# A recurrent layer whose states move from PSUM to SBUF, with rows staged by channel group and weights loaded in pieces

## The chip, the cores and the metric

The kernel runs on one NeuronCore of a Trainium2 chip. The metric is device time in microseconds. A core has five engines that run side by side: TensorE (PE, matrix products), VectorE (DVE), ScalarE (ACT), GpSimd (POOL) and SyncE (SP, which here only issues DMAs). They wait for each other through semaphores. SBUF is the working memory; PSUM is the small memory into which TensorE writes, and GpSimd does not touch it.

## What is computed

Two transformer-like layers over 32 sequences of 192 tokens (64 from images, 128 from text), 256 channels wide. The first has attention and a ternary feed-forward net. The second has a recurrent mixer with 512 inner channels and then a mixture of 8 experts. The change touches the recurrent mixer and the loads of the experts' weights. From the reference, cut to the mixer:

```python
xz = einsum('btd,ed->bte', x, Win)
xi, z = split(xz, 2, axis=-1)
lam = exp(-C * softplus(omega) * sigmoid(xi @ Wl.T + bl))
v = xi @ Wv.T + bv
h0 = xi[:, 0]
def step(h_prev, inp):
    x_t, v_t, lam_t = inp
    vh = sum(v_t * h_prev, axis=-1, keepdims=True)
    vv = sum(v_t * v_t, axis=-1, keepdims=True)
    Qh = h_prev - 2.0 * v_t * (vh / vv)
    h = lam_t * Qh + (1.0 - lam_t) * x_t
    return (h, h)
# h = all states, one after the other over t
out = einsum('bti,di->btd', silu(z) * h, Wout)
```

Every time step needs the state of the step before it, so the 192 steps form one chain.

## The kernel before

The program has three parts, one after the other: `part_a` (embedding and the first layer), `part_b` (the recurrent mixer) and `part_c` (the experts). The change is in `part_b`, apart from one number in `part_c`.

`part_b` works in 48 tiles of 4 time steps. A tile is 32 sequences x 4 steps = 128 rows. Every engine runs the same loop over `i`, from -5 to 50, and in pass `i` it does what each stage of the pipeline needs: tile `i` is in the scan, tile `i + 3` is being projected, tile `i - 1` is being turned into outputs.

The stages of tile `j` are these. TensorE projects the normed rows onto four things of 512 columns each (`l`, `v`, `xi`, `z`), each split in high and low parts for precision. ACT and DVE make from them four rows of 512 values: `U` (the scaled v), `LAM` (the decay), `DRIVE` and `GATE`, and write them to the tile `B_stage` in SBUF. There a partition is a row (sequence and step). The scan needs another layout: a partition is a sequence and one of 4 groups of 128 channels, and the steps lie behind each other. So SP issues four DMAs of 256 KB, one per channel group, from `B_stage` to the ring `B_scan_in` (4 tiles deep).

The scan itself runs on DVE and TensorE. For step `t` DVE does four operations on 128 x 128 values:

- `products(t)`: U times the previous state, summed along the free axis into one partial dot per partition (`B_partial_dots`, L1187),
- `decayed(t)`: LAM times the previous state (L1189),
- `driven(t)`: minus DRIVE (L1192),
- `stepped(t)`: plus `B_decayed_u` times the full dot (L1203).

Between the first and the last of them TensorE sums the partial dots over the four channel groups with one small product (L1296). The first three operations of step `t + 1` are issued right behind the last of step `t` (function `ahead`), so the scan comes in groups of four DVE operations: `stepped(t)`, `products(t+1)`, `decayed(t+1)`, `driven(t+1)`. Between the groups DVE does the other work of the pass: B_residual (L1215) and the GATE row (L1221) after the first, B_log_decay (L1231) and the statistics (L1237, L1240) after the second, B_y_lo (L1245) and B_x_lo (L1252) after the third, the DRIVE row (L1265) after the fourth. All of these have at most one input in SBUF that is wide; the other comes from PSUM.

The states lie in PSUM, in two banks that take turns (`STATE + j % 2`). When a tile is through, ACT copies its four states to `B_states` in SBUF (L1110), and GpSimd multiplies them with the gate into `B_y` (L1036). GpSimd also makes `B_decayed_u` = LAM x U for the next tile (L1048), and some operations on one value per partition. All engines take their work strictly in the written order, so one that waits holds up all that is behind it.

The experts' first two weight matrices and the small constants of `part_c` are loaded during `part_b`, in pass `TT - 18` = 30, all at one point of the SP queue.

Of the kernel before, what the change touches and what calls it, by code (L numbers as in the profile page):

```python
# [846 lines left out]
def part_b(nc, W, E, io, consts):  # L847
# [3 lines left out]
    with ExitStack() as ctx:  # L851
# [28 lines left out]
        stage = sb("B_stage", [P, 2, 4, DI])  # L880
# [11 lines left out]
        TURN, OUT, STATE, DOT = 3, 4, 5, 7  # L892
# [4 lines left out]
        def state(j, k):  # L897
            return ps[:, STATE + j % 2, k * P:(k + 1) * P]
# [62 lines left out]
        def _(sp):  # L961
# [13 lines left out]
            for i in range(FIRST, LAST):  # L975
                if i == TT - 18:
                    for a, b in ((E.b_up, io["up_bias"]), (E.b_dn, io["down_bias"])):
                        sp.dma_start(a[:], b).then_inc(E.s["const_in"], 16)
# [712 lines left out]
```

## Time and profile before

| what | value |
|---|---|
| median of 3 runs | 997.94 us (995.04 to 998.17) |
| the profiled execution, own time | 999.17 us |
| its span | 997.4 us |
| PE busy | 942.3 us, 94% |
| DVE busy | 785.9 us, 79% |
| ACT busy | 594.5 us, 60% |
| POOL busy | 542.2 us, 54% |
| TensorE clock over the span | 0.983 of full |
| moved by DMA | 96.34 MB in 135878 packets |

The rows come from one profiled execution; its own time is 1.8 us above its span. Busy time of matrix products overlaps, since they are pipelined, so a busy TensorE is not one at its peak. Durations of neighbouring DVE operations overlap a little too: an operation that need not wait starts some 0.08 us before the end of the one ahead of it.

### The profile page before, as it was taken

The numbers are of one execution on the slowest core, as the hardware profiler recorded it, in microseconds if no ns is written. First come the engines' busy times: TensorE is split into PE (matmuls) and PEld (weight loads), VectorE is DVE, ScalarE is ACT, GpSimd is POOL, SyncE is SP. The second block draws the span as 40 slices with busy tenths as digits, with TensorE's granted clock in tenths as the row PEclk, the third lists the DMA queues.
The fourth block names the chain that finished last, engine by engine and source line by source line (L and its number), as shares of the span: only waits on it lengthen the run. The fifth ranks groups of instructions, "written<-read, shape, count | busy, mean of one in ns | idle before, by whom it ended". The sixth has DMA issues, their size and how long they took to land. (4 is left out here: it accounts for less than half of the span.)

```text
span 997.4 us, 19802 instructions
## 1 busy us (share of the span) xinstructions
PE 942.3 (94%) x6006; PEld 844.9 (85%) x6006; DVE 785.9 (79%) x2396; ACT 594.5 (60%) x1181; POOL 542.2 (54%) x662
## 2 busy tenths in 40 slices
PE   6889999999999999988799999999998999997998
PEld 6789999999999999875588888888887888876887
DVE  4877777777777777664499999999997889995776
ACT  1366666666666666563567676777664666752541
POOL 4256666666666666344355455555543446542663
PEclk9999999999999999899899999999999899999999
DMA  6001111111111141003799999999999999993210
GB/s 221 17 27 43 44 43 43 42 42 42 42 42 42 42 149 32 17 17 111 89 149 156 156 156 154 156 154 155 155 154 173 145 153 145 150 143 76 98 64 22
DMA packets 135878, 96.34 MB, mean 97 GB/s; under 512 B 12270, under 2 KB 130166, under 8 KB 135158
## 3 DMA queue, kind: packets, MB, share of 16 engines
q1 hardware_dynamic: 134262, 91.20, 53.4%
q0 software_dynamic: 1536, 4.20, 1.4%
q8 instruction: 36, 0.59, 0.3%
q14 instruction: 44, 0.36, 0.2%
HBM read 31.91 MB, written 13.11 MB: 45 GB/s over the span
## 5 line engine op out<-in xcount | busy, mean ns | idle before, releaser
L334 POOL TENSOR_TENSOR gelu_lo<-gelu_out,gelu_hi 128x384 fp32r<-128x384 f32 x124 | 145.6, 1200 | 34.0 <-DVE gelu_hi L549 32.1
L1036 POOL TENSOR_TENSOR B_y<-B_scan_in,B_states 128x512 f32<-128x512 f32 x48 | 61.8, 1288 | 97.8 <-ACT B_states L1110 97.8
L752 PE MATMUL psAB<-ternary_down,gelu_hi 128*128 128x256 f32 x384 | 96.7, 290 | 4.9 <-POOL gelu_lo L334 4.0
L688 PE MATMUL psAB<-x2T_hi,ternary_up 128*128 128x384 f32 x256 | 94.9, 371 | 2.5 <-DVE residual L678 2.3
L752 PE MATMUL psAB<-ternary_down,gelu_lo 128*128 128x256 f32 x384 | 93.3, 282 | 0.0
L688 PE MATMUL psAB<-x2T_lo,ternary_up 128*128 128x384 f32 x256 | 87.9, 343 | 0.0
L1284 PE MATMUL psAB<-Win_hi,B_x_hi 128*128 128x512 f32 x192 | 83.5, 435 | 0.0
L1296 PEld LDWEIGHTS psAB<-B_partial_dots,B_minus_same_batch 128*128 128x128 f32 x384 | 65.3, 191 | 18.2 <-DVE B_partial_dots L1187 9.2
L752 PEld LDWEIGHTS psAB<-ternary_down,gelu_hi 128*128 128x128 f32 x384 | 72.2, 188 | 8.9 <-POOL gelu_lo L334 7.5
L1203 DVE SCALAR_TENSOR_TENSOR psAB<-B_decayed_u,psAB 128x128 f32<-128x128 f32 x192 | 68.0, 354 | 12.7 <-PE psAB L1296 11.5
L1284 PE MATMUL psAB<-Win_hi,B_x_lo 128*128 128x512 f32 x192 | 75.7, 394 | 0.0
L1284 PE MATMUL psAB<-Win_lo,B_x_hi 128*128 128x512 f32 x192 | 75.2, 392 | 0.0
L1048 POOL TENSOR_TENSOR B_decayed_u<-B_scan_in 128x512 f32<-128x512 f32 x48 | 62.0, 1291 | 24.0 <-DMA B_scan_in<-B_stage 16.8
L752 PEld LDWEIGHTS psAB<-ternary_down,gelu_lo 128*128 128x128 f32 x384 | 72.5, 189 | 0.0
L1042 POOL TENSOR_TENSOR B_v_scale<-B_half_vv,half_powers 128x1 f32<-128x1 f32 x48 | 26.3, 548 | 83.9 <-ACT B_v_squared L1131 79.3
L403 ACT ACTIVATE gelu_out<-psAB 128x384 f32<-128x384 f32 x128 | 62.6, 489 | 13.6 <-PE psAB L688 13.3
L1187 DVE CUSTOM_DVE_ANT_0 B_products<-B_scan_in,psAB 128x128 f32<-128x128 f32 x192 | 55.2, 287 | 19.0 <-DVE psAB L1203 7.8
L1192 DVE TENSOR_TENSOR psAB<-psAB,B_scan_in 128x128 f32<-128x128 f32 x192 | 57.4, 299 | 6.5
L568 DVE TENSOR_TENSOR gelu_sq_sum<-gelu_sq_sum,gelu_sq 128x384 f32<-128x384 f32 x105 | 61.1, 582 | 1.7
L1296 PE MATMUL psAB<-B_partial_dots,B_minus_same_batch 128*128 128x1 f32 x384 | 55.0, 212 | 7.3 <-DVE B_partial_dots L1187 7.1
L688 PEld LDWEIGHTS psAB<-x2T_hi,ternary_up 128*128 128x128 f32 x256 | 49.2, 192 | 11.6 <-ACT gelu_out L403 7.4
L1309 PE MATMUL psAB<-Wout_hi,B_y_hi 128*128 128x256 f32 x192 | 55.3, 288 | 2.7 <-DVE B_y_lo L1245 1.5
(267 smaller groups left out, 3330.4 us busy)
## 6 DMA issues: line engine op xcount, KB each, us to landing
B_scan_in<-B_stage SPq DMA_DIRECT2D x192, 256.0 KB, 6.6
patches<-in_patches SPq DMA_DIRECT2D x16, 384.0 KB, 3.1
B_residual<-layer_out SPq DMA_DIRECT2D x48, 128.0 KB, 3.5
out_dram<-B_residual SPq DMA_DIRECT2D x48, 128.0 KB, 2.8
layer_out<-residual SPq DMA_DIRECT2D x32, 128.0 KB, 1.8
raw_Win<-in_experts SPq DMA_DIRECT2D x4, 768.0 KB, 4.4
raw_Wl<-in_experts SPq DMA_DIRECT2D x4, 768.0 KB, 4.1
layer_out<-residual SPq DMA_DIRECT2D x32, 64.0 KB, 2.0
```

The source lines that it names most:

```text
L334: nc.gpsimd.tensor_tensor(act_l[:, k, :], act[:, k % DEEP, :], act_h[:, k, :].bitcast(F32), ALU.subtract).then_inc(s["ffn_lo"], 1)
L403: nc.scalar.activation(act[:, k % DEEP, :], ps[:, 6 + k % 2, 0:GT], ACT.Gelu).then_inc(s["gelu_done"], 1)
L568: nc.vector.tensor_tensor(sqsum[:], sqsum[:], sq[:, k % DEEP, :], ALU.add).then_inc(s["sqsum_done"], 1)
L688: last = nc.tensor.matmul(out, a, b, start=(n == 0), stop=(n == len(terms) - 1))
L752: last = nc.tensor.matmul(ps[:, 6 + k // 2, (k % 2) * D:(k % 2 + 1) * D], x[:, c, k * P:(k + 1) * P], dn_w[:, c, :], start=(c == 0 and x i ...
L1036: nc.gpsimd.tensor_tensor(y[:, j % 2], ring[:, j % R_RING, :, GATE, :], hs[:, j % 2], ALU.mult).then_inc(s["y"], 1)
L1048: nc.gpsimd.tensor_tensor(lu[:, j % 2], ring[:, j % R_RING, :, LAM, :], ring[:, j % R_RING, :, U, :], ALU.mult).then_inc(s["lu"], 1)
L1192: nc.vector.tensor_tensor(state(j, k), state(j, k), ring[:, j % R_RING, k, DRIVE, :], ALU.subtract).then_inc(s["scan"], 1)
L1203: nc.vector.scalar_tensor_tensor(out=state(i, k), in0=lu[:, i % 2, k, :], scalar=dot[:, t % 2:t % 2 + 1], in1=state(i, k), op0=ALU.mult, o ...
L1284: last = nc.tensor.matmul(out, a, b, start=(not biased and ks[0] == 0 and n == 0), stop=(ks[-1] == DC - 1 and n == len(terms) - 1), skip_g ...
L1296: nc.tensor.matmul(dot[:, t % 2:t % 2 + 1], minus[:], part[:, t % 2:t % 2 + 1], start=True, stop=True).then_inc(s["dot"], 1)
L1309: last = nc.tensor.matmul(ps[:, OUT, 0:D], *terms[n], start=(n == 0), stop=(n == len(terms) - 1))
```

## The change

There are three edits.

1. *Rows staged by channel group.* `B_stage` is laid out as group, row kind, channel instead of row kind, channel. The writes to it go through a view (`by_group`), and each of the four DMAs reads 2 KB in a piece per partition instead of four pieces of 512 B.
2. *Experts' inputs in small pieces.* The loads that stood at one point of the SP queue are spread over passes 22 to 36, one or two per pass, behind that pass's transfer to the scan; each weight matrix comes in four pieces of 192 KB.
3. *States in SBUF.* `state(j, k)` now is a part of `B_states`. ACT's copy and its semaphore go. GpSimd's B_y waits for the last step of the tile itself, and `ahead` waits for `y` before it writes over a tile of states. The two `tensor_tensor` of the scan become `scalar_tensor_tensor` with a factor of 1.0.

```diff
-        stage = sb("B_stage", [P, 2, 4, DI])
+        stage = sb("B_stage", [P, 2, IC, 4, P])
...
         def state(j, k):
-            return ps[:, STATE + j % 2, k * P:(k + 1) * P]
+            return hs[:, j % 2, k, :]
...
+        def by_group(ap):
+            return ap.rearrange("p (g c) -> p g c", g=IC)
...
-                if i == TT - 18:
-                    for a, b in ((E.b_up, io["up_bias"]), (E.b_dn, io["down_bias"])):
-                        sp.dma_start(a[:], b).then_inc(E.s["const_in"], 16)
...
-                    sp.wait_ge(s["w_lo"], 3)
-                    sp.wait_ge(s["m_ps"], 2)
-                    for e in range(2):
-                        sp.dma_start(E.raw[e], io["experts"][e]).then_inc(E.s["raw_in%d" % e], 16)
...
                     for g in range(IC):
                         sp.dma_start(ring[g * NB:(g + 1) * NB, j % R_RING].rearrange("b r w c -> b (r w c)"),
-                                     stage[:, j % 2, :, g * P:(g + 1) * P]).then_inc(arrived[j % 4], 16)
+                                     stage[:, j % 2, g, :, :].rearrange("p w c -> p (w c)")).then_inc(arrived[j % 4], 16)
+
+
+                if i == TT - 26:
+                    sp.dma_start(E.b_up[:], io["up_bias"]).then_inc(E.s["const_in"], 16)
+                    sp.dma_start(E.b_dn[:], io["down_bias"]).then_inc(E.s["const_in"], 16)
...
+                if i in range(TT - 19, TT - 11):
+                    if i == TT - 19:
+                        sp.wait_ge(s["w_lo"], 3)
+                        sp.wait_ge(s["m_ps"], 2)
+                    e, n = divmod(i - (TT - 19), 4)
+                    cols = slice(n * 6 * D // 4, (n + 1) * 6 * D // 4)
+                    sp.dma_start(E.raw[e][:, cols], io["experts"][e][:, cols]).then_inc(E.s["raw_in%d" % e], 16)
...
-                    pool.wait_ge(s["hs"], j + 1)
+                    pool.wait_ge(s["scan"], stepped(4 * j + 3))
...
-                if has(i - 1):
-                    j = i - 1
-                    sc.wait_ge(s["scan"], decayed(4 * j + 4) if j + 1 < TT else stepped(4 * j + 3))
-                    wait(sc, s["y"], j - 1)
-                    nc.scalar.activation(hs[:, j % 2].rearrange("p a b -> p (a b)"), ps[:, STATE + j % 2, :],
-                                         ACT.Copy).then_inc(s["hs"], 1)
...
-                    wait(v, s["hs"], j - 1)
+                    wait(v, s["y"], j - 1)
...
-                nc.vector.tensor_tensor(state(j, k), ring[:, j % R_RING, k, LAM, :], previous(j, k),
-                                        ALU.mult).then_inc(s["scan"], 1)
+                nc.vector.scalar_tensor_tensor(out=state(j, k), in0=ring[:, j % R_RING, k, LAM, :], scalar=1.0,
+                                               in1=previous(j, k), op0=ALU.mult, op1=ALU.mult).then_inc(s["scan"], 1)
                 v.wait_ge(s["scan"], decayed(t))
-                nc.vector.tensor_tensor(state(j, k), state(j, k), ring[:, j % R_RING, k, DRIVE, :],
-                                        ALU.subtract).then_inc(s["scan"], 1)
+                nc.vector.scalar_tensor_tensor(out=state(j, k), in0=state(j, k), scalar=1.0,
+                                               in1=ring[:, j % R_RING, k, DRIVE, :], op0=ALU.mult,
+                                               op1=ALU.subtract).then_inc(s["scan"], 1)
```

The order of the work on DVE stays. What its operations read and write changes, and one wait. These are the rows of DVE where one tile of the scan ends and the next begins, with the semaphores that each waits for. psAB is PSUM, all other names are in SBUF; ISA is the operation of L1187. Before:

```order
L1203 SCALAR_TENSOR_TENSOR psAB<-B_decayed_u,psAB 128x128 [waits B_dot,B_scan]
L1187 ISA B_products,B_partial_dots<-B_scan_in,psAB 128x128 [waits B_scan,B_hs,B_arrived3]
L1187 ISA B_partial_dots 128x1
L1189 TENSOR_TENSOR psAB<-B_scan_in,psAB 128x128
L1192 TENSOR_TENSOR psAB<-psAB,B_scan_in 128x128 [waits B_scan]
L1265 SCALAR_TENSOR_TENSOR B_stage<-B_stage,psAB 128x512 [waits B_xi,B_lam]
```

And of the changed kernel:

```order
L1205 SCALAR_TENSOR_TENSOR B_states<-B_decayed_u,psAB,B_states 128x128 [waits B_dot,B_scan]
L1188 ISA B_products,B_partial_dots<-B_scan_in,B_states 128x128 [waits B_scan,B_y,B_arrived3]
L1188 ISA B_partial_dots 128x1
L1190 SCALAR_TENSOR_TENSOR B_states<-B_scan_in,B_states 128x128
L1193 SCALAR_TENSOR_TENSOR B_states<-B_states,B_scan_in 128x128 [waits B_scan]
L1267 SCALAR_TENSOR_TENSOR B_stage<-B_stage,psAB 128x4x128 [waits B_xi,B_lam]
```

Each of the four operations of a step read one wide tensor from PSUM and one from SBUF before, and reads two from SBUF now (psAB in the first row is the dot, one value per partition). The wait for B_hs became one for B_y.

The second place is the SP queue in pass 30, where the loads for the experts stand. Before, from the transfer of the pass ahead to that of the pass itself:

```order
L1020 DMA B_scan_in<-B_stage 32x16x128 x4
L978 DMA C_up_bias<-in_up_bias 128x32
L978 DMA C_down_bias<-in_down_bias 8x256
L984 DMA C_picked<-in_picked 128x2 x2
L984 DMA C_picked<-in_picked 64x2 x4
L984 DMA C_routing<-in_routing 128x8 x2
L984 DMA C_routing<-in_routing 64x8 x4
L988 DMA raw_Win<-in_experts 128x1536
L988 DMA raw_Wl<-in_experts 128x1536
L1010 DMA out_dram<-B_residual 32x4x256
L964 DMA B_residual<-layer_out 128x1x256
L1020 DMA B_scan_in<-B_stage 32x16x128 x4
```

And of the changed kernel, at the same pass:

```order
L1010 DMA B_scan_in<-B_stage 32x4x512 x4
L1028 DMA raw_Win<-in_experts 128x384
L1000 DMA out_dram<-B_residual 32x4x256
L967 DMA B_residual<-layer_out 128x1x256
L1010 DMA B_scan_in<-B_stage 32x4x512 x4
L1028 DMA raw_Win<-in_experts 128x384
```

Sixteen transfers that stood ahead of one tile's inputs are gone from there; one small piece stands behind each tile's inputs instead.

## Rows read from the trace of the kernel before

**Rows 1.** Busy time by engine (operations), clock, DMA share, GB/s, mid-layer.

```profile
600.00:700.00 100.00, 100.00 (x589) 86.09 (x587) 92.51 (x329) 69.44 (x141) 50.35 (x83) 1.00 1.05 155
```

**Rows 2.** Timeline of DVE, one tile: start, length, operation, idle before.

```profile
640.45 0.36 DVE L1203 SCALAR_TENSOR_TENSOR psAB<-B_decayed_u,psAB 128x128 f32<-128x128 f32 x1 [0.21 <-PE psAB L1296]
...
641.38 0.30 DVE L1192 TENSOR_TENSOR psAB<-psAB,B_scan_in 128x128 f32<-128x128 f32 x1
...
644.79 0.35 DVE L1203 SCALAR_TENSOR_TENSOR psAB<-B_decayed_u,psAB 128x128 f32<-128x128 f32 x1
...
646.85 0.35 DVE L1203 SCALAR_TENSOR_TENSOR psAB<-B_decayed_u,psAB 128x128 f32<-128x128 f32 x1
647.37 0.29 DVE L1187 CUSTOM_DVE_ANT_0 B_products<-B_scan_in,psAB 128x128 f32<-128x128 f32 x1 [0.17 <-DVE psAB L1203]
...
647.59 0.29 DVE L1189 TENSOR_TENSOR psAB<-B_scan_in,psAB 128x128 f32<-128x128 f32 x1
647.91 0.30 DVE L1192 TENSOR_TENSOR psAB<-psAB,B_scan_in 128x128 f32<-128x128 f32 x1
648.12 0.68 DVE L1265 SCALAR_TENSOR_TENSOR B_stage<-B_stage,psAB 128x512 f32<-128x512 f32 x1
649.01 0.36 DVE L1203 SCALAR_TENSOR_TENSOR psAB<-B_decayed_u,psAB 128x128 f32<-128x128 f32 x1 [0.21 <-PE psAB L1296]
```

**Rows 3.** Timeline of GpSimd in the same tile.

```profile
641.46 1.28 POOL L1036 TENSOR_TENSOR B_y<-B_scan_in,B_states 128x512 f32<-128x512 f32 x1 [2.37 <-ACT B_states L1110]
...
644.81 1.29 POOL L1048 TENSOR_TENSOR B_decayed_u<-B_scan_in 128x512 f32<-128x512 f32 x1
...
647.48 0.19 POOL L1060 TENSOR_TENSOR B_shift<-B_minus_mean,B_rstd 128x1 f32<-128x1 f32 x1
```

**Rows 4.** Groups by shape (busy us, mean ns), then B_y's line (min/median/max ns).

```profile
L568 DVE TENSOR_TENSOR gelu_sq_sum<-gelu_sq_sum,gelu_sq 128x384 f32<-128x384 f32 x105 | 61.1, 582 | 1.7
L1192 DVE TENSOR_TENSOR psAB<-psAB,B_scan_in 128x128 f32<-128x128 f32 x192 | 57.4, 299 | 6.5
L549 DVE CAST gelu_hi<-gelu_out 128x384 fp32r<-128x384 f32 x80 | 28.3, 369 | 3.9 <-ACT gelu_out L403 3.8
...
L1036 POOL TENSOR_TENSOR B_y<-B_scan_in,B_states x48: 1270/1287/1299, 505.2 to 910.8; 128x512 f32<-128x512 f32 x48
```

**Rows 5.** Timelines of POOL and DVE where both use SBUF, three places.

```profile
66.89 3.23 POOL L334 TENSOR_TENSOR gelu_lo<-gelu_out,gelu_hi 128x384 fp32r<-128x384 f32 x2 [1.26 <-DVE gelu_hi L549]
...
419.92 1.26 POOL L334 TENSOR_TENSOR gelu_lo<-gelu_out,gelu_hi 128x384 fp32r<-128x384 f32 x1 [3.81 <-DVE gelu_hi L549]
...
419.76 0.55 DVE L568 TENSOR_TENSOR gelu_sq_sum<-gelu_sq_sum,gelu_sq 128x384 f32<-128x384 f32 x1
420.23 1.17 DVE L549 CAST gelu_hi<-gelu_out 128x384 fp32r<-128x384 f32 x1
...
926.91 3.48 POOL L1422 TENSOR_TENSOR C_w_lo<-raw_Win,C_w_hi 128x1536 fp32r<-128x1536 f32 x1
...
929.47 2.08 DVE L1523 SCALAR_TENSOR_TENSOR C_glu<-C_up,C_silu 128x512 f32<-128x512 f32 x2
```

**Rows 6.** Timelines of SP's queue and DVE, and two us by windows.

```profile
754.48 3.50 SPq L984 DMA_DIRECT2D C_routing<-in_routing  x6
...
760.83 3.65 SPq L1020 DMA_DIRECT2D B_scan_in<-B_stage  x4
...
760.21 0.36 DVE L1203 SCALAR_TENSOR_TENSOR psAB<-B_decayed_u,psAB 128x128 f32<-128x128 f32 x1 [0.18 <-PE psAB L1296]
...
773.12 0.29 DVE L1187 CUSTOM_DVE_ANT_0 B_products<-B_scan_in,psAB 128x128 f32<-128x128 f32 x1 [6.15 <-DMA B_scan_in<-B_stage]
...
785.68 0.36 DVE L1203 SCALAR_TENSOR_TENSOR psAB<-B_decayed_u,psAB 128x128 f32<-128x128 f32 x1 [0.38 <-PE psAB L1296]
...
773.00:775.00 2.00, 0.62 (x3) 0.57 (x3) 1.45 (x6) 1.88 (x4) 1.62 (x3) 0.50 1.24 169
```

**Rows 7.** Timeline of GpSimd late in the layer.

```profile
837.56 3.51 POOL L1064 TENSOR_TENSOR C_w_lo<-raw_Win,C_w_hi 128x1536 fp32r<-128x1536 f32 x1
```

More of the change, by code:

```diff
@@ L891, in part_b @@
         MERGE = (0, 1, 2, 3)
[L892 removed]
+        TURN, OUT, DOT = 3, 4, 7
         def bank(what, j):
@@ L908, in part_b @@
                 stats aggr ve rstd shift applied xT x_hi x_lo l v xi z tanh_l log_decay lam vsq rs u drive
-                tanh_z gate lu scan dot hs y yT y_hi y_lo wout res""".split():
+                tanh_z gate lu scan dot y yT y_hi y_lo wout res""".split():
             s[name] = ctx.enter_context(nc.semaphore("B_" + name))
@@ L1020, in _ @@
                         sp.dma_start(ring[g * NB:(g + 1) * NB, j % R_RING].rearrange("b r w c -> b (r w c)"),
-                                     stage[:, j % 2, :, g * P:(g + 1) * P]).then_inc(arrived[j % 4], 16)
+                                     stage[:, j % 2, g, :, :].rearrange("p w c -> p (w c)")).then_inc(arrived[j % 4], 16)
+                if i == TT - 26:
+                    sp.dma_start(E.b_up[:], io["up_bias"]).then_inc(E.s["const_in"], 16)
+                    sp.dma_start(E.b_dn[:], io["down_bias"]).then_inc(E.s["const_in"], 16)
+                if i in range(TT - 25, TT - 19):
+                    q, lo, hi, q_in, lo_in = ((0, 0, P, 0, 0), (2, 0, P, 3, 0), (1, 0, 64, 1, 64), (1, 64, P, 2, 0),
+                                              (3, 0, 64, 1, 0), (3, 64, P, 2, 64))[i - (TT - 25)]
+                    for a, b in ((E.picked, io["picked"]), (E.weights, io["routing"])):
+                        sp.dma_start(a[lo:hi, q, :], b[lo_in:lo_in + hi - lo, q_in, :]).then_inc(E.s["const_in"], 16)
+                if i in range(TT - 19, TT - 11):
[5 more added lines that the diff above has]
+                    sp.dma_start(E.raw[e][:, cols], io["experts"][e][:, cols]).then_inc(E.s["raw_in%d" % e], 16)
         @block.gpsimd
@@ L1155, in _ @@
                     sc.wait_ge(s["rs"], j + 1)
[L1156 removed]
+                    nc.scalar.activation(stage[:, j % 2, :, U, :], by_group(ps[:, bank("v", j), :]), ACT.Copy,
                                          scale=rs[:, j % 2:j % 2 + 1]).then_inc(s["u"], 1)
                     sc.wait_ge(s["log_decay"], j + 1)
[L1159 removed]
+                    nc.scalar.activation(stage[:, j % 2, :, LAM, :], by_group(u2[:]), ACT.Exp).then_inc(s["lam"], 1)
                     if has(j + 1):
@@ L1220, in _ @@
                     v.wait_ge(s["tanh_z"], j + 1)
-                    nc.vector.scalar_tensor_tensor(out=stage[:, j % 2, GATE, :], in0=th_z[:], scalar=1.0,
-                                                   in1=ps[:, bank("z", j), :], op0=ALU.add,
+                    nc.vector.scalar_tensor_tensor(out=stage[:, j % 2, :, GATE, :], in0=by_group(th_z[:]), scalar=1.0,
+                                                   in1=by_group(ps[:, bank("z", j), :]), op0=ALU.add,
                                                    op1=ALU.mult).then_inc(s["gate"], 1)
@@ L1260, in _ @@
                     if j == 0:
-                        nc.vector.tensor_scalar(stage[:, 0, LAM, :], stage[:, 0, LAM, :], first[:], None,
+                        nc.vector.tensor_scalar(stage[:, 0, :, LAM, :], stage[:, 0, :, LAM, :], first[:], None,
                                                 ALU.mult).then_inc(s["first_ready"], 1)
@@ L1264, in _ @@
                     v.wait_ge(s["xi"], j + 1)
-                    nc.vector.scalar_tensor_tensor(out=stage[:, j % 2, DRIVE, :], in0=stage[:, j % 2, LAM, :], scalar=1.0,
-                                                   in1=ps[:, bank("xi", j), :], op0=ALU.subtract,
+                    nc.vector.scalar_tensor_tensor(out=stage[:, j % 2, :, DRIVE, :], in0=stage[:, j % 2, :, LAM, :], scalar=1.0,
+                                                   in1=by_group(ps[:, bank("xi", j), :]), op0=ALU.subtract,
                                                    op1=ALU.mult).then_inc(s["drive"], 1)
```

10 lines of the change are left out of this document (2 added, 8 removed).

## The prediction, made before the changed kernel had run

> **What bounds the kernel now.** I read the page's busy table first, then one long stretch of the recurrent layer by windows, then one tile of it as a timeline on the vector engine and on GpSimd, then the places where DVE and GpSimd both want SBUF, and last the one place where the scan stops. The recurrent layer is 48 tiles of 4 time steps. In a stretch in its middle TensorE is busy 100.00 of 100 us and DVE 92.51 [rows 1]. Two engines are full, and the reader is to see which has slack. A tile lasts 649.01 - 640.45 = 8.56 us (48 of them are 411 of the 997 us), and within it DVE waits for TensorE once, 0.21 us, in front of the tile's first step [rows 2]. Everything else on DVE is one chain: step, product, decay, subtraction, then an operation of another kind, four times over. So TensorE sets the pace, and DVE follows with only 0.21 us to spare per tile. Whatever adds more than that to DVE's tile sets a new pace.
>
> GpSimd is half idle. Per tile it runs two wide operations, B_y at 641.46 and B_decayed_u at 644.81, and some tiny ones [rows 3]. The 48 B_y took 1270 to 1299 ns [rows 4]: nothing DVE did beside them mattered, and all that DVE did beside them had at most one input in SBUF, the other in PSUM.
>
> **What the change adds: two SBUF inputs.** The states move from PSUM to SBUF. Then all four operations of a step read two SBUF tensors: 16 operations per tile that meet B_y and B_decayed_u, which read SBUF too. The trace shows what such a meeting costs [rows 5]. At 929.47 DVE starts two C_glu operations (512 wide, both inputs in SBUF) while GpSimd is inside a C_w_lo that ends at 926.91 + 3.48 = 930.39. A 512-wide operation of this kind lasts 0.68 us [rows 2], and a next one starts some 0.08 before its end, so the pair should take 1.28; it took 2.08. DVE stood for 0.80 us, until about 0.12 us before GpSimd's end. It did not run slower beside GpSimd, it stood. The other way round, at 66.89 two GpSimd operations took 3.23 us together where at 419.92 one took 1.26. So one engine holds the port for nearly its whole operation: 1.29 - 0.13 = 1.16 us for B_y or B_decayed_u.
>
> The Trainium skill says this in the page "SBUF — State Buffer", section "Who interferes with whom": a DVE instruction with two SBUF inputs and a GpSimd instruction that reads SBUF shut each other out, and the first holds the pair for the whole instruction. The trace agrees but for the last 0.13 us; with the whole 1.29 the sum below would be 48 x 0.13 = 6 us larger.
>
> **Who gets the port.** At 419.76 a DVE addition (0.55) ran and a CAST followed at 420.23; GpSimd had asked at 419.92, and the CAST took 1.17 us where its group's mean is 369 ns [rows 4, 5]. If the addition frees the port 0.13 before its end at 420.31, GpSimd slipped into a gap of 0.05 us. In the scan chain the gaps are wider: the decay at 647.59 frees the port at 647.75 and the subtraction comes at 647.91, 0.16 later; step 3 ends at 647.20 and the product comes at 647.37 [rows 2]. So I take it that GpSimd gets in inside the chain, and a DVE operation behind it stands for 1.16 - 0.16 = 1.0 us.
>
> **The sum per tile.** *B_y.* Before, it waited for ACT's copy and began 1.01 us into the tile, beside operations that read PSUM. Now it waits for step 3 itself, which ends at 647.20, while GpSimd is free from 647.67 at the latest [rows 3]. So it is asked for inside the chain (product, decay, subtraction at 647.37 to 648.21), and costs 1.0 us. Lower bound: it has to wait until the subtraction ends, holds 648.08 to 649.24, and the next step, due at 649.01, loses 0.23. *B_decayed_u.* It starts at 644.81, and step 2 at 644.79: a tie today. In front of step 2 lie 1.1 us of DVE work that uses no second SBUF input. Once DVE is the late one, B_decayed_u, timed by TensorE and ACT, comes earlier against DVE and hides most of its 1.16 there. I take 0.2; bounds 0, and 1.0 if it always falls inside a chain. *Spare time:* 0.21 us is given back. *The operations themselves:* 384 wide with both inputs in SBUF, outside meetings, the group at line 568 has a mean of 582 ns including some meetings; the PSUM forms have 299 ns at 128 and 680 at 512 [rows 2, 4], so 550 at 384. I see no gain from SBUF and take 0 for the three-operand form too, since the 680 is of that form. Together 1.0 + 0.2 - 0.2 = 1.0 us per tile, 48 us in all (bounds 0.0 and 1.8: 0 and 86 us).
>
> The Trainium skill's page "VectorE: DVE Perf Modes", section "The TRN2 errata", puts the fixed part at 58 cycles from SBUF and 120 from PSUM. By it each of the 16 operations would be an estimated 0.065 us shorter, 1.0 us per tile, and the block would be paid back in full. The rows do not show it, and so it stands as a rival.
>
> **What the change removes.** The experts' weights now come as one load of 192 KB in each of eight tiles instead of two of 768 KB and fourteen small ones in one go. Today the SP queue is busy with the small ones past 754.48 + 3.50, the inputs of the next tiles are issued behind them at 760.83, and DVE waits 6.15 us for them at 773.12 [rows 6]. TensorE then comes back at a granted clock of 0.50, the lower level (1.2 GHz). From the first step at 760.21 to the one at 785.68 two tiles take 25.47 instead of 17.12 us: 8.35 lost, of which the wait is 6.15 and the rest the low clock and the catching up. With pieces, and with B_stage sent as 2 KB instead of 512 B runs, I take all of it as gained: -8.35 (bound: 6.15 of it at least). The DMA share in the steady stretch, 1.05 [rows 1], falls, but no one waits for it there: worth 0. The copy on ACT (48 times) is hidden behind B_y's slack: 0. Added: C_w_lo (3.51 us at 837.56 [rows 7]) now holds the port too, some 3.4 us against at most 1.1 of DVE work that does not need it, +2.3; from that go some 1.3 us for hitches there that now hide behind DVE: +1.
>
> Sum: 999.17 (the profiled execution: span 997.4 and 1.8 around it) + 48 - 8.35 + 1 = 1039.8. The profiled execution lies 1.2 above the median 997.94, so 1038.6, say **1038 us**.
>
> **Rivals.**
> *B: GpSimd gets the port only between the groups of four.* For it: at 66.89 GpSimd was held off over several DVE operations in a row [rows 5]; against it: the CAST at 420.23, and wider gaps here. Then B_y costs 0.23, B_decayed_u up to 0.7 where it arrives ahead of step 2, say 0.4; less 0.21 it is 0.45 per tile, 21 us: 998 + 21 - 7 = 1012 (1003 to 1028).
> *C: faster.* The block is paid by something: shorter operations from SBUF, or both GpSimd operations landing in the port-free stretches. Place: the first step of each tile; price: the stall's 8.35 us against 48 tiles, so it decides at 8.35/48 = 0.17 us of net delay per tile. Below that the kernel is faster, down to 998 - 9 = 989. Against it: the spare 0.21, B_y's lower bound 0.23 and the tie at 644.8.
> *D: the stall stays* (the pieces collide with other loads) and the block comes: 1047.
> *E: they cancel*, 995 to 1001.
>
> **Chances.** A (the forecast, own range 1020 to 1060) 0.52, B 0.25, C 0.14, D 0.04, E 0.05. Within 0.3% (3 us) is about what a measurement here can tell from no change. Slower: A + B + D = 0.81; same 0.05; faster 0.14. The range leaves out C and E (0.19): 1003 to 1060.
>
> **What would show it.** Right: in the middle of the layer a tile of about 9.5 us instead of 8.56; TensorE waiting for B_partial_dots once or twice per tile; single DVE scan operations of 1.2 to 1.4 us among those of 0.3, always beside B_y or B_decayed_u; B_y starting within 0.1 us of step 3's end or as soon as the shift is done; no wait for B_scan_in near 766 us; TensorE's clock at its upper level there. Wrong: scan operations of 0.30 us throughout beside a running B_y (then C); long ones only as first of a group (then B); or GpSimd operations grown to 2.5 us while DVE keeps its pace, which would mean that DVE always wins the port and only GpSimd pays.

## The result, and the profile after

The changed kernel takes 1065.14 us (median of 4 runs, 1061.57 to 1069.31); the kernel before took 997.85 beside it. The ratio is 1.0682 with a 95% interval of 1.0628 to 1.0737: slower by 6.8%. The forecast was 1038 with a range of 1003 to 1060. The sign and the kind of loss came as forecast; one of the two meetings at the port was priced far too low, and so the loss is 67 us and not 40. The profiled execution, from which the rows of this section come, took 1068.38 us, 3.2 above the median; its mean granted clock was 0.979, where the two quicker runs had 0.989.

The same stretch of the layer as in [rows 1], by windows (busy time of each engine, its operations, clock, DMA share, GB/s):

```profile
600.00:700.00 100.00, 93.45 (x499) 72.31 (x498) 95.59 (x277) 53.79 (x110) 43.95 (x68) 1.00 0.79 129
```

TensorE has fallen from 100.00 to 93.45 us of 100, and in the same time it does 499 products instead of 589. DVE has risen to 95.59 with fewer operations (277 for 329). The granted clock is 1.00 in both, the upper level (2.4 GHz), so the clock plays no part in this stretch. The profile page's groups of the vector operations of the scan and of the weight load behind them say where the time sits (busy us, mean ns, then idle time before and what ended it):

```profile
L1188 DVE CUSTOM_DVE_ANT_0 B_products<-B_scan_in,B_states 128x128 f32<-128x128 f32 x192 | 105.4, 549 | 13.0 <-DVE B_states L1205 7.9
L1298 PEld LDWEIGHTS psAB<-B_partial_dots,B_minus_same_batch 128*128 128x128 f32 x384 | 58.7, 191 | 65.1 <-DVE B_partial_dots L1188 63.3
L1205 DVE SCALAR_TENSOR_TENSOR B_states<-B_decayed_u,psAB,B_states 128x128 f32<-128x128 f32 x192 | 102.6, 534 | 2.0 <-PE psAB L1298 1.3
```

A mean of 549 ns hides two sorts of operation. The vector operations that touch B_states and GpSimd's B_y, by line (min/median/max ns), show that most are as short as before, and that GpSimd's own operations are not longer:

```profile
L1188 DVE CUSTOM_DVE_ANT_0 B_products<-B_scan_in,B_states x192: 284/292/1355, 493.3 to 975.9; 128x128 f32<-128x128 f32 x192
L1190 DVE SCALAR_TENSOR_TENSOR B_states<-B_scan_in,B_states x192: 279/285/1373, 493.5 to 976.1; 128x128 f32<-128x128 f32 x192
L1193 DVE SCALAR_TENSOR_TENSOR B_states<-B_states,B_scan_in x192: 291/292/1416, 493.8 to 976.4; 128x128 f32<-128x128 f32 x192
L1205 DVE SCALAR_TENSOR_TENSOR B_states<-B_decayed_u,psAB,B_states x192: 341/350/3400, 494.2 to 977.2; 128x128 f32<-128x128 f32 x192
L1043 POOL TENSOR_TENSOR B_y<-B_scan_in,B_states x48: 1262/1292/1361, 502.0 to 977.7; 128x512 f32<-128x512 f32 x48
```

The timeline of DVE, from the first step of one tile (644.32) over its step 3 (651.47) and the first step of the next tile (654.39) to the step 2 of that one (658.73), and that of GpSimd beside it:

```profile
644.32 0.35 DVE L1205 SCALAR_TENSOR_TENSOR B_states<-B_decayed_u,psAB,B_states 128x128 f32<-128x128 f32 x1
...
651.47 0.35 DVE L1205 SCALAR_TENSOR_TENSOR B_states<-B_decayed_u,psAB,B_states 128x128 f32<-128x128 f32 x1
651.99 1.34 DVE L1188 CUSTOM_DVE_ANT_0 B_products<-B_scan_in,B_states 128x128 f32<-128x128 f32 x1 [0.17 <-DVE B_states L1205]
...
653.79 0.68 DVE L1267 SCALAR_TENSOR_TENSOR B_stage<-B_stage,psAB 128x512 f32<-128x512 f32 x1
654.39 0.35 DVE L1205 SCALAR_TENSOR_TENSOR B_states<-B_decayed_u,psAB,B_states 128x128 f32<-128x128 f32 x1
...
658.73 1.09 DVE L1205 SCALAR_TENSOR_TENSOR B_states<-B_decayed_u,psAB,B_states 128x128 f32<-128x128 f32 x1
```

```profile
651.90 1.29 POOL L1043 TENSOR_TENSOR B_y<-B_scan_in,B_states 128x512 f32<-128x512 f32 x1 [0.58 <-DVE B_states L1205]
657.86 0.55 POOL L1049 TENSOR_TENSOR B_v_scale<-B_half_vv,half_powers 128x1 f32<-128x1 f32 x1 [4.67 <-ACT B_v_squared L1132]
658.38 1.30 POOL L1055 TENSOR_TENSOR B_decayed_u<-B_scan_in 128x512 f32<-128x512 f32 x1
```

B_y starts 0.08 us after step 3 ends (651.82) and 0.09 before the product; the product then takes 1.34 instead of 0.29: a block of 1.05, as the time for which a DVE operation stands is called here. B_decayed_u starts at 658.38, 0.35 before step 2, and step 2 takes 1.09 instead of 0.35: a block of 0.74. Together 1.79; the 0.21 that DVE used to wait at the tile's first step [rows 2] comes off: 1.58. The tile has in fact grown from 8.55 to 10.08 us, by 1.53, and stays there from the third tile on, apart from three tiles around ACT's C_w_hi and GpSimd's C_w_lo and the last two.

### The profile page after: what moved, and what is told of

Read it like the earlier page. It is cut to its first block and busy times, and to the rows that moved or that the text cites. A ratio compares the mean times of both kernels' runs of the same rounds, so it can differ in the third digit from the quotient of the medians.

```text
span 1066.6 us, 19714 instructions
## 1 busy us (share of the span) xinstructions
PE 981.3 (92%) x6006; PEld 843.4 (79%) x6006; DVE 869.9 (82%) x2396; ACT 569.5 (53%) x1133; POOL 548.9 (51%) x662
## 5 line engine op out<-in xcount | busy, mean ns | idle before, releaser
L1188 DVE CUSTOM_DVE_ANT_0 B_products<-B_scan_in,B_states 128x128 f32<-128x128 f32 x192 | 105.4, 549 | 13.0 <-DVE B_states L1205 7.9
L1298 PEld LDWEIGHTS psAB<-B_partial_dots,B_minus_same_batch 128*128 128x128 f32 x384 | 58.7, 191 | 65.1 <-DVE B_partial_dots L1188 63.3
L1205 DVE SCALAR_TENSOR_TENSOR B_states<-B_decayed_u,psAB,B_states 128x128 f32<-128x128 f32 x192 | 102.6, 534 | 2.0 <-PE psAB L1298 1.3
L1112 ACT ACTIVATE psAB<-B_channel_rows 128x512 f32<-128x512 f32 x48 | 28.9, 602 | 114.5 <-DVE B_stage L1267 114.5
L1298 PE MATMUL psAB<-B_partial_dots,B_minus_same_batch 128*128 128x1 f32 x384 | 68.6, 248 | 22.7 <-DVE B_partial_dots L1188 20.8
L1311 PE MATMUL psAB<-Wout_hi,B_y_hi 128*128 128x256 f32 x192 | 58.7, 306 | 19.0 <-DVE B_x_lo L1254 16.4
L1311 PEld LDWEIGHTS psAB<-Wout_hi,B_y_hi 128*128 128x128 f32 x192 | 36.9, 192 | 37.8 <-DVE B_y_lo L1247 37.0
L1193 DVE SCALAR_TENSOR_TENSOR B_states<-B_states,B_scan_in 128x128 f32<-128x128 f32 x192 | 57.2, 298 | 6.6
```

The source lines that it names most:

```text
L1188: nc.vector.tensor_tensor_reduce(prod[:], ring[:, j % R_RING, k, U, :], previous(j, k), 1.0, 0.0, ALU.mult, ALU.add, part[:, t % 2:t % 2 + ...
L1205: nc.vector.scalar_tensor_tensor(out=state(i, k), in0=lu[:, i % 2, k, :], scalar=dot[:, t % 2:t % 2 + 1], in1=state(i, k), op0=ALU.mult, o ...
L1298: nc.tensor.matmul(dot[:, t % 2:t % 2 + 1], minus[:], part[:, t % 2:t % 2 + 1], start=True, stop=True).then_inc(s["dot"], 1)
L1311: last = nc.tensor.matmul(ps[:, OUT, 0:D], *terms[n], start=(n == 0), stop=(n == len(terms) - 1))
```

## Experiments

Each was compared with the kernel before on the same chip. Diffs are against the changed kernel unless said otherwise, and line numbers differ by a few from kernel to kernel. First the results at a glance; the tile is that of the middle of the layer. The kernel before took 997.85 us beside the changed kernel and 994.82 to 995.60 beside the others, so the ratios say more than the differences of the times. narrow_y and the three whose names begin with tiny leave out part of the computation.

| kernel | us | ratio to before, 95% interval | tile, us |
|---|---|---|---|
| before | 997.85 | 1 | 8.55 |
| changed | 1065.14 | 1.0682 [1.0628, 1.0737] | 10.08 |
| stage_only | 995.15 | 1.0000 [0.9987, 1.0013] | 8.55 |
| pieces_only | 988.68 | 0.9937 [0.9917, 0.9957] | 8.55 |
| stage_and_pieces | 989.11 | 0.9933 [0.9915, 0.9951] | 8.55 |
| states_only | 1067.10 | 1.0713 [1.0694, 1.0731] | 10.09 |
| two_operand | 1064.16 | 1.0694 [1.0676, 1.0712] | 10.09 |
| narrow_y | 1043.44 | 1.0463 [1.0441, 1.0484] | 9.68 |
| tiny_y | 1042.52 | 1.0463 [1.0440, 1.0485] | 9.68 |
| tiny_decayed_u | 1028.64 | 1.0336 [1.0311, 1.0361] | 9.34 |
| tiny_both | 991.92 | 0.9969 [0.9952, 0.9986] | 8.59 |
| y_placed | 1042.92 | 1.0480 [1.0455, 1.0504] | 9.67 |
| both_placed | 1019.42 | 1.0227 [1.0198, 1.0257] | 8.7 to 9.8 |
| y_and_u_late | 998.35 | 1.0038 [1.0025, 1.0052] | 8.67 |

### Which edit does what

**stage_and_pieces**: edits 1 and 2 of the section on the change, without edit 3. As a diff against the changed kernel it puts the states back:

```diff
-            return hs[:, j % 2, k, :]
+            return ps[:, STATE + j % 2, k * P:(k + 1) * P]
...
-                    pool.wait_ge(s["scan"], stepped(4 * j + 3))
+                    pool.wait_ge(s["hs"], j + 1)
...
```

> The kernel before with the first two edits alone: rows staged by channel group, loads in pieces; the states stay in PSUM and ACT copies them. Theory P (the port: the loss comes only from DVE operations with two SBUF inputs meeting GpSimd's wide ones): no loss is left and the stall near 766 us is gone, so about 8 us less than before, 990 us, tiles of 8.56 us throughout. Theory S (the new staging layout or the pieces cost DVE or the DMA queue time, and the states only part of it): clearly above 998 us.

**states_only**: edit 3 alone, the same lines the other way round in the kernel before.

> The kernel before with the third edit alone: states in SBUF, B_y waits for the last step, no copy on ACT. P: the tile of 10.09 us as in the changed kernel, and the stall at the experts' loads is hidden or partly hidden behind the slower pace, so 1065 to 1073 us. S: well below 1060.

Measured: 989.11 and 1067.1. All of the loss is edit 3. The two tiles at the experts' loads take 11.43 and 11.26 instead of 10.09 in states_only, where they took 14.75 and 10.72 before. So beside a scan that DVE paces, the pile of loads costs only 1.34 + 1.17 = 2.5 us.

**stage_only** and **pieces_only** take edits 1 and 2 apart. Against the kernel before, the first has

```diff
-        stage = sb("B_stage", [P, 2, 4, DI])
+        stage = sb("B_stage", [P, 2, IC, 4, P])
...
-                                     stage[:, j % 2, :, g * P:(g + 1) * P]).then_inc(arrived[j % 4], 16)
+                                     stage[:, j % 2, g, :, :].rearrange("p w c -> p (w c)")).then_inc(arrived[j % 4], 16)
...
```

and the second has the loads at `i in range(TT - 19, TT - 11)` in place of those at `i == TT - 18`.

> The kernel before with the first edit alone (rows staged by channel group, 2 KB runs). If the stall near 766 us is a matter of DMA time, the shorter transfers shrink it: the experts' two loads of 768 KB still stand ahead of the scan's inputs, so some 2 to 6 us of the 8.35 are gained, 992 to 996 us. If it is a matter of the fifteen issues on SP's queue ahead of it, nothing: 998 us.

> The kernel before with the second edit alone (loads in pieces, 512 B runs stay). The DMA share in the steady stretch is 1.05 already, so pieces of 192 KB add about 5% per tile for eight tiles. Either they are hidden in the slack of 6.6 us to landing (990 us), or each of eight tiles is late by up to 0.5 us (990 to 994 us). No stall at 766 us in both.

What DVE waited for between 740 and 800 us (total, times, longest), in stage_only:

```profile
DVE B_products L1190 <- DMA B_scan_in<-B_stage: 6.0, 1, 6.0
DVE psAB L1206 <- PE psAB L1299: 2.7, 7, 1.1
```

and in pieces_only:

```profile
DVE psAB L1206 <- PE psAB L1299: 1.4, 7, 0.2
DVE B_products L1190 <- DVE psAB L1206: 1.2, 7, 0.2
```

The wait of 6.0 us stays with the staging alone and is gone with the pieces alone. Staging by channel group cuts the packets of the execution from 135878 to 62150 and the DMA share in the middle of the layer from 1.05 to 0.91, and the time does not move: 1.0000, interval ±0.0013. The whole gain of 0.6% is the pieces'. So the shorter transfers did not shrink the stall, and the second reading of stage_only's expectation stands. The SP queue of the kernel before shows it too:

```profile
746.13 3.78 SPq L1020 DMA_DIRECT2D B_scan_in<-B_stage  x4
749.96 0.63 SPq L978 DMA_DIRECT2D C_up_bias<-in_up_bias  x1
```

The transfers to the scan were issued 8.55 us apart (737.58, 746.13), so the next was due at 754.68. The sixteen loads kept the queue from 749.96 to 759.07, and it came at 760.83 [rows 6], 6.15 late. That the two loads of 768 KB (issued in 0.96 us of this) also delay the data is not excluded: no run takes them apart from the fourteen small ones.

**two_operand**: the decay and the subtraction as `tensor_tensor` again.

```diff
-                nc.vector.scalar_tensor_tensor(out=state(j, k), in0=ring[:, j % R_RING, k, LAM, :], scalar=1.0,
-                                               in1=previous(j, k), op0=ALU.mult, op1=ALU.mult).then_inc(s["scan"], 1)
+                nc.vector.tensor_tensor(state(j, k), ring[:, j % R_RING, k, LAM, :], previous(j, k),
+                                        ALU.mult).then_inc(s["scan"], 1)
...
-                nc.vector.scalar_tensor_tensor(out=state(j, k), in0=state(j, k), scalar=1.0,
-                                               in1=ring[:, j % R_RING, k, DRIVE, :], op0=ALU.mult,
-                                               op1=ALU.subtract).then_inc(s["scan"], 1)
+                nc.vector.tensor_tensor(state(j, k), state(j, k), ring[:, j % R_RING, k, DRIVE, :],
+                                        ALU.subtract).then_inc(s["scan"], 1)
```

> The changed kernel with the two operations of the scan that were turned into scalar_tensor_tensor written as tensor_tensor again, on the same SBUF operands. P: the form is of no account, both have two SBUF inputs; 1065 us within 3, operations within 15 ns of 285. Rival F (the three-operand form is what is slow, or what helps): a change of over 5 us one way or the other.

The tile is 10.09 and the time 1064.16: the form is of no account.

### Taking the meetings away

**narrow_y**: B_y for one of the four steps.

```diff
+            nc.gpsimd.memset(y[:], 0.0)
...
-                    nc.gpsimd.tensor_tensor(y[:, j % 2], ring[:, j % R_RING, :, GATE, :], hs[:, j % 2],
+                    nc.gpsimd.tensor_tensor(y[:, j % 2, 0:1], ring[:, j % R_RING, 0:1, GATE, :], hs[:, j % 2, 0:1],
                                             ALU.mult).then_inc(s["y"], 1)
```

> The changed kernel, in which GpSimd multiplies only one of the four steps of a tile with its gate (B_y 128 wide instead of 512; the other three quarters of B_y stay zero). Its length should fall from 1.29 to about 0.43 us, from the 1.005 us of 384 and 1.29 of 512 elements, so its hold of the port to 0.30. P: the product that stands behind it takes 0.5 instead of 1.34 us, the tile 9.25 instead of 10.09, the kernel about 1065 - 40 = 1025 us. S (states in SBUF are slow for DVE by themselves): 1065 us, since nothing on DVE changes.

Its tile is 9.68, 0.41 shorter, where 0.84 was expected, and the time 1043.44 and not 1025. B_y (0.46 us) does block only 0.22. But step 2 and B_decayed_u now come at the same moment. DVE, then GpSimd:

```profile
653.00 1.44 DVE L1207 SCALAR_TENSOR_TENSOR B_states<-B_decayed_u,psAB,B_states 128x128 f32<-128x128 f32 x1
```

```profile
653.00 1.30 POOL L1057 TENSOR_TENSOR B_decayed_u<-B_scan_in 128x512 f32<-128x512 f32 x1
```

GpSimd wins the tie and step 2 takes 1.44 instead of 1.09: -0.83 + 0.35 = -0.48. With the 0.07 that DVE waits again at the tile's first step (B_stage ends at 648.66, the step starts at 648.65 and not 0.08 before that end) this is the -0.41 seen. Half of what is taken off one meeting comes back at the other. So the two were then removed singly and together, by making 16 of the 512 columns only. Tiny_both has both parts of this diff, and tiny_y and tiny_decayed_u have one each:

```diff
+            nc.gpsimd.memset(y[:], 0.0)
+            nc.gpsimd.memset(lu[:], 0.0)
...
-                    nc.gpsimd.tensor_tensor(y[:, j % 2], ring[:, j % R_RING, :, GATE, :], hs[:, j % 2],
-                                            ALU.mult).then_inc(s["y"], 1)
+                    nc.gpsimd.tensor_tensor(y[:, j % 2, 0, 0:16], ring[:, j % R_RING, 0, GATE, 0:16],
+                                            hs[:, j % 2, 0, 0:16], ALU.mult).then_inc(s["y"], 1)
...
-                    nc.gpsimd.tensor_tensor(lu[:, j % 2], ring[:, j % R_RING, :, LAM, :], ring[:, j % R_RING, :, U, :],
-                                            ALU.mult).then_inc(s["lu"], 1)
+                    nc.gpsimd.tensor_tensor(lu[:, j % 2, 0, 0:16], ring[:, j % R_RING, 0, LAM, 0:16],
+                                            ring[:, j % R_RING, 0, U, 0:16], ALU.mult).then_inc(s["lu"], 1)
```

> The changed kernel with B_y and B_decayed_u made by GpSimd for 16 of their 512 columns only; the rest of both is zero, so most of these two products is left out. Theory (the two meetings at the port are all of the loss): the blocks of 1.05 and 0.74 us shrink to at most 0.1 each, the vector engine's tile is 10.08 - 1.05 - 0.74 = 8.29 to 8.5 us, TensorE sets the pace again at 8.55, and the time is that of the kernel with the loads in pieces alone, 988.7 (986 to 993). Rival 1 (states in SBUF cost something besides the meetings, on ACT, TensorE or in the vector operations): tile above 8.65, more than 995. Rival 2 (the three-operand operations from SBUF are quicker): the same time, but the vector engine waits for TensorE by about 1.2 us per tile (0.21 before plus 16 x 0.065) instead of 0.1 to 0.4.

> The changed kernel with B_y alone made for 16 of its 512 columns; the rest of B_y is zero. If the blocks simply added up, the tile would be 10.08 - 1.05 = 9.03 us and the time 1065 - 50 = 1015. By what the narrow B_y showed, B_decayed_u then meets step 2 head on and takes 1.05 to 1.09 there instead of 0.74: tile 9.35 to 9.45, time 1030 to 1035.

> The changed kernel with B_decayed_u alone made for 16 of its 512 columns; the rest of B_decayed_u is zero. B_y still starts within 0.1 us of step 3's end whatever comes before it, so its block stays 1.05 and the term of B_decayed_u goes whole: tile 10.08 - 0.74 = 9.34 (9.3 to 9.45), time 1065 - 35 = 1030 (1027 to 1034). This is the size that the forecast gave to B_y alone. Rival: with B_decayed_u gone another meeting grows (B_y held longer): above 1040.

| | B_decayed_u gone | B_decayed_u whole |
|---|---|---|
| B_y gone | 8.59 us, 991.9 | 9.68 us, 1042.5 |
| B_y whole | 9.34 us, 1028.6 | 10.08 us, 1065.1 |

With both gone, TensorE is busy 100.00 us of 100 again although all states are in SBUF (tiny_both, by windows):

```profile
600.00:700.00 100.00, 100.00 (x584) 85.66 (x584) 92.36 (x326) 62.94 (x127) 26.12 (x80) 1.00 0.93 153
```

So the two meetings are all of the loss in the steady stretch but for 0.04 us per tile. What is left against pieces_only is 3.2 us: these 0.04, and C_w_lo, which still blocks a step. DVE waits 0.19 us for TensorE at the tile's first step and not 1.2, so rival 2 falls too. B_y alone costs 0.75 over 8.59, B_decayed_u alone 1.09, both together 1.49: they do not add up. tiny_decayed_u came as expected. tiny_y missed: a tile of 9.68 and 1042.5 where 9.35 to 9.45 and 1030 to 1035 stood. Its step 2 takes 1.45 and DVE waits 0.20 for TensorE again at the tile's first step; I had left that wait out of the sum. DVE:

```profile
651.97 1.45 DVE L1207 SCALAR_TENSOR_TENSOR B_states<-B_decayed_u,psAB,B_states 128x128 f32<-128x128 f32 x1
...
656.42 0.68 DVE L1269 SCALAR_TENSOR_TENSOR B_stage<-B_stage,psAB 128x512 f32<-128x512 f32 x1
657.30 0.36 DVE L1207 SCALAR_TENSOR_TENSOR B_states<-B_decayed_u,psAB,B_states 128x128 f32<-128x128 f32 x1 [0.20 <-PE psAB L1300]
```

and GpSimd, over two tiles:

```profile
651.97 1.30 POOL L1057 TENSOR_TENSOR B_decayed_u<-B_scan_in 128x512 f32<-128x512 f32 x1
...
661.13 0.55 POOL L1051 TENSOR_TENSOR B_v_scale<-B_half_vv,half_powers 128x1 f32<-128x1 f32 x1 [5.33 <-ACT B_v_squared L1134]
661.65 1.29 POOL L1057 TENSOR_TENSOR B_decayed_u<-B_scan_in 128x512 f32<-128x512 f32 x1
```

### Placing the meetings

**y_placed**: B_y waits for the decay of the next tile's second step, so that it is held until the subtraction ends and lies under B_residual and B_stage.

```diff
-                    pool.wait_ge(s["scan"], stepped(4 * j + 3))
+                    pool.wait_ge(s["scan"], decayed(4 * j + 5) if j + 1 < TT else stepped(4 * j + 3))
```

> The changed kernel, B_y waits for the decay of the next tile's second step instead of the last step of its own, so that it gets the port when the subtraction behind that decay is through, in front of B_residual and the GATE row. P: it then holds the port until 1.32 us after the subtraction's start, step 1 comes 1.14 after it: block 0.18 instead of 1.05. Tile 10.09 - 0.87 = 9.2 us, kernel about 1026 us. S (the cost is not in the meeting): 1065 us, or more since B_y is later.

**both_placed**: the same, and in GpSimd's order B_decayed_u ahead of B_v_scale, with a wait of its own.

```diff
                     wait_arrived(pool, j)
+                    if has(i):
+                        pool.wait_ge(s["scan"], decayed(4 * i + 2))
                     nc.gpsimd.tensor_tensor(lu[:, j % 2], ring[:, j % R_RING, :, LAM, :], ring[:, j % R_RING, :, U, :],
```

> As y_placed, and B_decayed_u is put ahead of B_v_scale in GpSimd's order and waits for the decay of step 2, so that it runs under B_log_decay and the statistics, 1.36 us until step 2. P: its block of 0.74 goes to 0, DVE needs 8.35 + 0.18 = 8.53 us per tile, TensorE sets the pace again with 8.56, the kernel comes to about 990 us with states in SBUF. If the waits of B_v_scale behind it matter, some us more. S: above 1040.

y_placed missed: a tile of 9.67 and 1042.92 where 9.2 and about 1026 stood. It behaves like narrow_y and tiny_y: B_y costs 0.10 where 0.18 was expected, and B_decayed_u, just ahead of step 2, costs 1.0 where the 0.74 had been left as it was. GpSimd, then DVE:

```profile
651.21 1.30 POOL L1055 TENSOR_TENSOR B_decayed_u<-B_scan_in 128x512 f32<-128x512 f32 x1
```

```profile
651.31 1.35 DVE L1205 SCALAR_TENSOR_TENSOR B_states<-B_decayed_u,psAB,B_states 128x128 f32<-128x128 f32 x1
```

Both_placed missed by 29 us (1019.42 for about 990) and shows why the order on GpSimd was what it was. Its waits between 560 and 740 us:

```profile
POOL B_y L1043 <- DVE B_states L1192: 50.1, 19, 2.9
ACT B_stage L1159 <- POOL B_v_scale L1057: 26.0, 20, 3.0
...
POOL B_decayed_u L1051 <- DMA B_scan_in<-B_stage: 14.8, 9, 2.4
```

ACT stands for B_v_scale, which now comes behind B_decayed_u; so B_stage is full later, its transfer starts later, and B_decayed_u waits for the transfer and comes late itself. The tiles are uneven, 8.7 to 9.8 us.

**y_and_u_late** keeps GpSimd's order and has B_decayed_u wait for the decay in front of step 3.

```diff
+                    if has(i):
+                        pool.wait_ge(s["scan"], decayed(4 * i + 3))
```

> The changed kernel, whole computation; B_y waits for the decay of the next tile's second step and B_decayed_u for the decay of step 3, so both should begin as their chain's subtraction ends. The order on GpSimd stays (B_v_scale ahead of B_decayed_u). B_y then costs 0.1 as measured; B_decayed_u holds the port for 1.16 from the end of the subtraction while B_y_lo and B_x_lo (1.05 us together, one SBUF input each) run: 0.1 to 0.25 in front of step 3. The vector engine's tile is 8.29 + 0.1 + 0.2 = 8.6 to 8.7, time 991 to 998. Rival: the operations on GpSimd behind B_decayed_u (B_rstd, B_shift) come 1 us or more later, ACT and TensorE wait for them and the tiles become uneven, as with both placed: above 1005.

GpSimd over one tile:

```profile
647.60 1.40 POOL L1043 TENSOR_TENSOR B_y<-B_scan_in,B_states 128x512 f32<-128x512 f32 x1 [1.14 <-DVE B_states L1192]
650.45 0.55 POOL L1049 TENSOR_TENSOR B_v_scale<-B_half_vv,half_powers 128x1 f32<-128x1 f32 x1 [1.46 <-ACT B_v_squared L1134]
652.13 1.32 POOL L1057 TENSOR_TENSOR B_decayed_u<-B_scan_in 128x512 f32<-128x512 f32 x1 [1.13 <-DVE B_states L1192]
```

and DVE behind each of the two (in the tile ahead for B_decayed_u, which began at 643.48 there):

```profile
644.49 0.45 DVE L1207 SCALAR_TENSOR_TENSOR B_states<-B_decayed_u,psAB,B_states 128x128 f32<-128x128 f32 x1
...
648.69 0.45 DVE L1207 SCALAR_TENSOR_TENSOR B_states<-B_decayed_u,psAB,B_states 128x128 f32<-128x128 f32 x1
```

Each costs 0.10 us, the tile is 8.67 as expected, and the kernel takes 998.35 (ratio 1.0038, 1.0025 to 1.0052), 0.35 above the expected range. Two waits take back 67 of the 76 us that lie between the changed kernel and pieces_only. Of the 9.7 that are left, 48 x 0.12 = 5.8 are the steady tiles, and the tiles around C_w_lo, which still blocks a step, have 2.9. So no version with states in SBUF beats pieces_only (988.68) or stage_and_pieces (989.11), the two whole computations that beat both kernels.

## Why the prediction was wrong

**What sets the pace** was right. DVE with 0.21 us to spare became the bound; TensorE now waits for B_partial_dots 63.3 us in all at its weight load. The 0.21 was given back, and is there again (0.20) as soon as B_y is out of the way.

**B_y: 1.0 us** was right. The trace has 1.05, and tiny_decayed_u, in which it is the only wide operation that meets the scan, has a tile of 9.34 = 8.55 + 1.05 - 0.21 within 0.05. The hold is right as well: the product ended at 653.33, so by its usual 0.29 it began at 653.04, 0.15 before B_y's end at 653.19, and the port was shut for 1.14 us where 1.16 was taken.

**B_decayed_u: 0.2 us** is the step that failed. It costs 0.74 in the changed kernel and 1.0 to 1.1 where B_y blocks little or nothing ahead of it (y_placed, narrow_y, tiny_y). I had argued that "once DVE is the late one, B_decayed_u, timed by TensorE and ACT, comes earlier against DVE and hides most of its 1.16 there". It came earlier, but by 0.35 us, where a cost of 0.2 needs 1.16 - 0.2 = 0.96. It is not timed by TensorE and ACT as by a clock of their own: these take their start from DVE. ACT's timeline of the changed kernel:

```profile
654.50 0.60 ACT L1112 ACTIVATE psAB<-B_channel_rows 128x512 f32<-128x512 f32 x1 [2.55 <-DVE B_stage L1267]
...
657.02 0.60 ACT L1132 ACTIVATE B_v_squared<-psAB 128x512 f32<-128x512 f32 x1 [0.62 <-PE psAB L1286]
```

DVE's B_stage ends at 654.47; ACT's prefill starts at 654.50; TensorE follows; ACT squares v at 657.02; GpSimd makes B_v_scale at 657.86 and B_decayed_u at 658.38. That is 3.91 us behind B_stage, and step 2 is 4.26 behind it. In the kernel before the first distance was 644.81 + 8.56 - 648.80 = 4.57 [rows 2, 3], and step 2 lay 4.55 behind; in tiny_y both are 661.65 - 657.10 = 4.55. A longer tile moves both together. Only B_y's block, which lies ahead of B_stage in the changed kernel, shortens the first distance, by 0.66, while step 2's falls by 0.29 with the wait of 0.21. That it is a block ahead of B_stage that does it is seen in B_v_scale, right behind which B_decayed_u runs. It starts 4.04 us behind the end of B_stage in the kernel before, 4.02 to 4.05 in tiny_y, tiny_both and y_placed, where B_y blocks nothing ahead of B_stage, 3.9 in y_and_u_late, where B_decayed_u's block of 0.10 lies ahead of B_stage, 3.81 in narrow_y with a block of 0.22, and 3.39 and 3.41 in the changed kernel and in tiny_decayed_u, both with the whole block. From tiny_decayed_u, DVE and then GpSimd:

```profile
649.32 0.68 DVE L1269 SCALAR_TENSOR_TENSOR B_stage<-B_stage,psAB 128x512 f32<-128x512 f32 x1
```

```profile
653.41 0.55 POOL L1051 TENSOR_TENSOR B_v_scale<-B_half_vv,half_powers 128x1 f32<-128x1 f32 x1 [4.69 <-ACT B_v_squared L1134]
```

Why a block there shortens the way over ACT and TensorE (perhaps because they get other work done meanwhile) is not shown. That the tie returns without it, three kernels show: narrow_y (653.00 and 653.00), tiny_y (651.97 and 651.97), and y_placed (651.21 and 651.31, the difference being B_y's 0.10 in step 1). I had the tie in front of me in [rows 2, 3], 644.81 and 644.79, and took it for a coincidence.

**The range** was cut too short by the same step. The bounds of the sum ran to 1.8 us per tile, which is 998 - 7 + 86 = 1077; the measured 1.53 lies inside them, and the range stopped at 1060. That 1065 would have been inside the bounds is no merit: the upper one supposed B_decayed_u inside a chain, and it blocked step 2.

**No gain from SBUF, none or loss from the form: 0** was right. The four operations of a step in the kernel before, by line (min/median/max ns):

```profile
L1187 DVE CUSTOM_DVE_ANT_0 B_products<-B_scan_in,psAB x192: 280/287/290, 495.4 to 908.4; 128x128 f32<-128x128 f32 x192
L1189 DVE TENSOR_TENSOR psAB<-B_scan_in,psAB x192: 290/290/297, 495.6 to 908.6; 128x128 f32<-128x128 f32 x192
L1192 DVE TENSOR_TENSOR psAB<-psAB,B_scan_in x192: 298/299/300, 496.0 to 908.9; 128x128 f32<-128x128 f32 x192
L1203 DVE SCALAR_TENSOR_TENSOR psAB<-B_decayed_u,psAB x192: 340/353/361, 496.4 to 909.7; 128x128 f32<-128x128 f32 x192
```

Their medians of 287, 290, 299 and 353 ns stand against 292, 285, 292 and 350 after (shown above): 10 ns less in all four together. Two_operand shows the form to be of no account.

The Trainium skill's page "VectorE: DVE Perf Modes", section "The TRN2 errata", would have had each shorter by an estimated 0.065 us; no run here shows that, and with it rival C falls. The rule that the prediction quoted from the Trainium skill's page "SBUF — State Buffer", section "Who interferes with whom", agrees with the traces of these runs, again but for the last part of the hold, 0.15 us here.

**The stall: -8.35** is right in the tiles against the kernel before: those of 14.75 and 10.72 are gone. In time it was at most a little too large: pieces_only gains 0.63%, 6.3 us, interval 4.3 to 8.3. It is not a gain that the pieces would have with the states in SBUF: there, by states_only, 2.5 us.

**C_w_lo: +1** was too low. It blocks a step for 3.05 us where 2.3 was counted, since it starts 0.21 before that step and not 1.1, the tile behind it is 0.95 longer, and that of ACT's C_w_hi, which goes ahead of it, 0.43:

```profile
883.67 3.46 POOL L1071 TENSOR_TENSOR C_w_lo<-raw_Win,C_w_hi 128x1536 fp32r<-128x1536 f32 x1
883.88 3.40 DVE L1205 SCALAR_TENSOR_TENSOR B_states<-B_decayed_u,psAB,B_states 128x128 f32<-128x128 f32 x1
```

Together 4.4 over the steady tile, against 2.4 before: +2.0.

**What was left out**: the last two tiles. They took 7.26 and 6.82 us before, with less work of the other kinds in them, and 9.53 and 10.02 now: 5.5 longer, 2.4 more than two ordinary ones. The first has two blocks, 1.06 and 1.03. The second has blocks of 0.69 and 1.03, and DVE waits for TensorE in front of B_residual, 1.97 us where it waited 0.40 before:

```profile
964.01 0.42 DVE L1217 SCALAR_TENSOR_TENSOR B_residual<-psAB,B_residual 128x256 f32<-128x256 f32 x1 [1.97 <-PE psAB L1311]
```

Put together, the misses are 48 x (1.53 - 1.00) = 25.4 us, of B_decayed_u above all, 1.0 of C_w_lo and 2.4 of the last tiles, less 2.1 by which the scan began earlier: 26.7, beside the 27.1 us between 1038 and 1065.14. That they meet so closely is in part luck, since the tiles are read from an execution 3.2 us above the median.

**Rivals.** B (the port only between groups) falls with the product of 1.34 us behind step 3: GpSimd got in inside the chain. D falls, since the tiles of 14.75 and 10.72 are 10.09 and 10.08 now; C and E fall by the time.

## What to carry to other kernels

Before a tensor that a chain of short vector operations works on is moved from PSUM to SBUF, list GpSimd's wide SBUF operations in the same period: each may cost the chain nearly its whole length, and here a wait that made each begin where the vector engine ran some 1 us of work with one SBUF input brought it down to 0.1 us. To say where an operation will fall when the pace changes, follow what releases it back until the chain meets the engine that sets the new pace; if it does, the two keep their distance, and a tie before is a tie after, unless a new block falls on the way between them. Test each edit of a bundle by itself: here one of three was worth 0.6%, one nothing, and the third lost 7%.

## What the runs showed of the hardware that was not expected

- Who gets the port is settled by very little. B_y, 0.09 us ahead of the product, shut it out for 1.05; at a tie in the trace (653.00, 651.97) GpSimd went first each time, and step 2 stood for 1.1.
- GpSimd's operation is as long as ever where it comes first and blocks the vector engine (1.29 us for B_y in the changed kernel), and longer where it comes second: 1.40 where it was released while a subtraction was running (647.60 in y_and_u_late).
- Runs of 2 KB instead of 512 B in the transfers to the scan halve the packets (135878 to 62150). Their median time to landing stays at 6.6 us, and the kernel's time changes by no more than 0.13%.
